# The second MLP product in token order, with the row chain behind the gates

## The reference

```python
h = tok(x)                                    # einsum bhid,oi,od->bho
h = h + attn_block(layernorm(h))              # linear attention, then the MLP:
#   x = x + attn;  h2 = ln(x)*g2 + beta2
#   x = x + gelu(h2 @ w1 + b1) @ w2 + b2      # 256 -> 1024 -> 256
h = h + ffn(layernorm(h))                     # no scale or shift in this layernorm
# ffn: logits = x @ gate_w.T (8 experts and one shared)
#      up to 4 experts a token by a sparse mixer, a cumulative top-p and a capacity
#      of 1280 tokens an expert, counted in token order
#      shared expert: silu(x @ G) * (x @ U) @ Dn, weighted by its softmax share
#      routed experts: the same with their own weights, added to the rows
```

## Time and profile before

| | busy us | share of the span |
|---|---|---|
| TensorE products | 2390.9 | 87% |
| VectorE | 1896.1 | 69% |
| GpSimd | 1566.2 | 57% |
| ScalarE | 1464.7 | 53% |

### The profile page before, as it was taken

One profiled execution on the slowest core, in us unless ns is written; L12 is line 12 of the kernel. 1 busy time (PEld: TensorE's weight loads), 2 busy tenths in 40 slices (PEclk: granted clock), 3 DMA queues, 4 the chain that ended last, 5 costly groups with the idle time before them and its releaser, 6 DMA issues. The chain is left out here.

```text
span 2740.9 us, 61192 instructions
## 1 busy us (share of the span) xinstructions
PE 2390.9 (87%) x22832; PEld 1732.9 (63%) x22832; DVE 1896.1 (69%) x4174; ACT 1464.7 (53%) x2731; POOL 1566.2 (57%) x1546
## 2 busy tenths in 40 slices
PE   4799999999999999999999858889898898985664
PEld 3588888888888888888887724444444444443553
DVE  2577777777777777777777736787777777875443
ACT  3566666666666666666666534444443344432232
POOL 1465656565666656565656523665566556656566
PEclk8999999999999999999999979999999999998787
DMA  4121111111111111111110020211121111100676
GB/s 146 43 64 61 40 64 61 61 44 61 60 61 42 42 40 44 40 44 36 47 38 14 9 98 24 78 59 50 48 84 53 50 41 50 35 9 16 128 136 100
DMA packets 115060, 152.21 MB, mean 56 GB/s; under 512 B 16537, under 2 KB 75917, under 8 KB 114768
## 3 DMA queue, kind: packets, MB, share of 16 engines
q1 hardware_dynamic: 88880, 124.46, 14.2%
q0 software_dynamic: 23808, 21.74, 4.4%
q10 hardware_dynamic: 2080, 2.10, 0.2%
...
## 5 line engine op out<-in xcount | busy, mean ns | idle before, releaser
L952 POOL TENSOR_TENSOR qkl<-fz,qkh 128x512 f16<-128x512 f32 x256 | 307.7, 1202 | 308.0 <-DVE qkh L849 303.8
L1806 POOL DMA_INDIRECT slot_dram<-xt,slot_u x256 | 257.5, 1006 | 74.9 <-issue 74.7
L521 PE MATMUL pF<-nh,qk_h 128*128 128x256 f16 x1024 | 281.3, 275 | 8.1 <-DVE nl L836 4.4
L522 PE MATMUL pF<-nh,qk_l 128*128 128x256 f16 x1024 | 280.6, 274 | 0.0
L523 PE MATMUL pF<-nl,qk_h 128*128 128x256 f16 x1024 | 280.5, 274 | 0.0
L964 POOL TENSOR_TENSOR ol<-on,oh 128x256 f16<-128x256 f32 x256 | 171.9, 672 | 153.5 <-ACT oh L786 153.5
L971 POOL TENSOR_TENSOR kvl<-kvacc,kvh 128x260 f16<-128x260 f32 x192 | 150.2, 782 | 107.7 <-ACT kvh L794 107.7
L763 ACT ACTIVATE sh<-sm 128x512 f16<-128x512 f32 x256 | 159.3, 622 | 84.5 <-DVE sm L872 84.5
L1786 POOL TENSOR_TENSOR al<-az,ah 128x512 f16<-128x512 f32 x64 | 79.2, 1238 | 215.8 <-DVE ah L1579 215.8
L846 DVE SCALAR_TENSOR_TENSOR fz<-pF,ez 128x512 f32<-128x512 f32 x256 | 175.3, 685 | 30.5 <-ACT ez L746 28.4
L740 ACT ACTIVATE rz<-pF 128x512 f32<-128x512 f32 x256 | 150.8, 589 | 84.5 <-PE pF L523 79.9
...
...
## 6 DMA issues: line engine op xcount, KB each, us to landing
xs<-in_x SPq DMA_DIRECT2D x128, 256.0 KB, 2.6
...
```

The source lines that it names most:

```text
L521: pe.matmul(out, wh, mh, start=first, stop=False, skip_group_check=True)
L522: pe.matmul(out, wl, mh, start=False, stop=False, skip_group_check=True)
L952: nc.gpsimd.tensor_tensor(qkl[:, pair:pair + 2, cols], fz[:, n % 2, :, :], qkh[:, pair:pair + 2, cols], ALU.subtract).then_inc(fl_ready, 1)
L1806: nc.gpsimd.indirect_dma_start(io["slot_dram"], bass.IndirectOffsetOnAxis(slot_u[:, c, k:k + 1], 0), xt[:, i % 2, c, :], None, bounds_chec ...
```

## The change

- `w2` puts tokens on partitions: the stationary side is `gh`/`gl` of a chunk of tokens, the moving side a row of `w2`, into pY as the down product does. The residual goes in by eight fp32 products of `hx` with `ident_w` (64 times the identity) at the head of w2. The biases and scales are as before.
- ScalarE copies the sum out of PSUM to `ht` (two buffers). VectorE takes mean and variance of each token there by bn_stats and bn_aggr. `mean3`, `var3`, `hp`, `xc3`, `sq3` and `turn_sums` go. rs3 has four columns, not 512.
- `xn` is made in token order, its high half by ScalarE and its low half by GpSimd straight into `xt` (three buffers). `turn_rows` now transposes from `xt` to the feature order, and ScalarE copies that to `xf`, from where gates and logits read.
- The order: `rstd3` stands behind `scale2`, `norm3` between gates 1 and 2, the low halves (`low3`) behind gates 2 and 3, then `rows_ahead` with `hx` and `x1` of later sequences. `turn_rows` half 0 stands between k = 1 and k = 2 of the down product, half 1 behind it.
- The explicit load of the exp and ln tables moves from `rstd3` to `logits`.

```diff
-        hp = sb("hp", [DT, T])
-        xc3, sq3, ln3, rs3, xn = sb("xc3", [DT, T]), sb("sq3", [DT, T]), sb("ln3", [T]), sb("rs3", [T]), sb("xn", [DT, T])
-        xnh, xnl = sb("xnh", [DT, T], F16), sb("xnl", [DT, T], F16)
-        xt = sb("xt", [2, CH, ROW], U32)
-        ht = sb("ht", [CH, D])
+        ht = sb("ht", [2, CH, D])
+        st3, mv3 = sb("st3", [CH, 6]), sb("mv3", [CH, 2])
+        ln3, rs3, xn = sb("ln3", [CH]), sb("rs3", [CH]), sb("xn", [CH, D])
+        xt = sb("xt", [XT, CH, ROW], U32)
+        xf = sb("xf2", [2, DT, T], F16)
+        xnh, xnl = xf[:, 0, :, :], xf[:, 1, :, :]
...
+                s["sums3"](i)
...
+                s["rstd3"](i)
...
-                s["mean3"](i, before)
...
-                    s["gate_up"](i - 1, after, (1, 2))
-                s["var3"](i)
+                    s["gate_up"](i - 1, after, (1,))
+                s["norm3"](i)
+                if before:
+                    s["gate_up"](i - 1, after, (2,))
+                s["low3"](i, 0)
                 if before:
                     s["gate_up"](i - 1, after, (3,))
-                s["rstd3"](i)
+                s["low3"](i, 1)
+                s["rows_ahead"](i)
...
-                    s["down"](i - 1)
-                s["turn_rows"](i, before)
+                    s["down"](i - 1, (0, 1))
+                s["turn_rows"](i, before, 0)
+                if before:
+                    s["down"](i - 1, (2, 3))
+                s["turn_rows"](i, before, 1)
...
-                s["turn_sums"](i)
...
+                if js[0] == 0:
+                    if i == 1:
+                        pe.wait_ge(ht_ready, 2)
+                    elif i >= 2:
+                        pe.wait_ge(ob_ready, count(i, CH, -CH))
+                    pe.wait_ge(hx_ready, count(i, DT, DT))
+                    for c in range(CH):
+                        toks = slice(c * P, (c + 1) * P)
+                        for t in range(DT):
+                            at = c // 2 * D + t * P
+                            mm = pe.matmul(pY[c % 2][:, at:at + P], hx[:, t, toks], ident_w[:, :], start=c < 2 and t == 0,
+                                           stop=False, skip_group_check=True)
+                    mm.then_inc(hx_added, 1)
...
+                    for c in range(CH):
+                        toks = slice(c * P, (c + 1) * P)
+                        mm = three(pY[c % 2][:, c // 2 * D:(c // 2 + 1) * D], gh[:, j, toks], gl[:, j, toks],
+                                   w2_h[:, j, :], w2_l[:, j, :], False, j == FT - 1)
...
-                for t in range(DT):
-                    mm = pe.matmul(pL[:, :], ones[:, :], hp[:, t, :], start=(t == 0), stop=(t == DT - 1))
...
+                if js[0] == 0:
+                    pe.wait_ge(xf_ready, count(i, 2, 2))
...
-            def var3(i):
-                pe.wait_ge(sq3_ready, count(i, DT, DT))
-                pe.wait_ge(xc3_ready, count(i, DT, DT))
-                for t in range(DT):
-                    mm = pe.matmul(pL[:, :], ones[:, :], sq3[:, t, :], start=(t == 0), stop=(t == DT - 1))
-                mm.then_inc(var3_done, 1)
...
+            def down(i, ks):
+                pe.wait_ge(ht_ready, 2 * SEQS if i == SEQS - 1 else count(i + 1, 2, 2))
+                for k in ks:
...
+                pe.wait_ge(xf_ready, count(i, 2, 2))
+                if i > 0:
+                    pe.wait_ge(lg_ready, count(i, 1, 0))
...
-                    pe.wait_ge(xt_ready, count(i, 2, half + 1))
-                    for c in range(2):
-                        toks = slice((2 * half + c) * P, (2 * half + c + 1) * P)
-                        for t in range(DT):
-                            w = c * DT + t
-                            mm = pe.transpose(pA[half][:, w * P:(w + 1) * P], hp[:, t, toks], ident[:, :])
-                    mm.then_inc(ht_done, 1)
+            def turn_rows(i, before, half):
+                pe.wait_ge(xnh_ready, count(i, 2, half + 1))
+                pe.wait_ge(xnl_ready, count(i, 2, half + 1))
+                if before:
+                    pe.wait_ge(az_ready, count(i, ST, 0))
+                else:
+                    pe.wait_ge(xc2_ready, count(i + 1, DT, DT))
+                    pe.wait_ge(rs2_step, count(i + 1, 2, 1))
+                bank16 = pA[half][:, :].bitcast(F16)
+                for part in range(2):
+                    for t in range(DT):
+                        for c in range(2):
+                            w = (part * DT + t) * 2 + c
+                            words = slice((part * DT + t) * P // 2, (part * DT + t + 1) * P // 2)
+                            mm = pe.transpose(bank16[:, w * P:(w + 1) * P],
+                                              xt[:, i % XT, 2 * half + c, words].bitcast(F16), ident16[:, :])
+                mm.then_inc(xt_done, 1)
...
+            def sums3(i):
+                act.wait_ge(w2_done, count(i, 1, 1))
+                if i >= 2:
+                    act.wait_ge(ob_ready, count(i, CH, -CH))
+                for b in range(2):
+                    nc.scalar.activation(ht[:, i % 2, b:CH:2, :], pY[b][:, :].rearrange("p (c n) -> p c n", c=2), ACT.Copy,
+                                         scale=1 / W2_SCALE).then_inc(ht_ready, 1)
+
+            def rstd3(i):
+                act.wait_ge(mv3_ready, count(i, CH, CH))
+                nc.scalar.activation(ln3[:, :], mv3[:, :, 1], ACT.Ln, bias=EPS).then_inc(rs3_step, 1)
+                act.wait_ge(rs3_step, count(i, 2, 1))
+                if i > 0:
+                    act.wait_ge(xn_ready, count(i, CH, 0))
+                nc.scalar.activation(rs3[:, :], ln3[:, :], ACT.Exp, scale=-0.5).then_inc(rs3_step, 1)
+
+            def norm3(i):
+                if i >= XT:
+                    act.wait_ge(rows_sent, count(i - XT + 1, 16 * CH * TOP, 0))
+                    act.wait_ge(xt_done, count(i - XT, 2, 2))
+                for half in range(2):
+                    act.wait_ge(xn_ready, count(i, CH, 2 * half + 2))
+                    nc.scalar.activation(xt[:, i % XT, 2 * half:2 * half + 2, 0:D // 2].bitcast(F16),
+                                         xn[:, 2 * half:2 * half + 2, :], ACT.Copy).then_inc(xnh_ready, 1)
...
-            def rstd3(i):
-                exp_ln_tables(nc, act)
-                act.wait_ge(var3_done, count(i, 1, 1))
-                nc.scalar.activation(ln3[:, :], pL[:, :], ACT.Ln, bias=EPS).then_inc(rs3_step, 1)
...
-
+                exp_ln_tables(nc, act)
...
-                    act.wait_ge(xt_done, count(i, 2, half + 1))
-                    if i >= 2:
-                        act.wait_ge(rows_sent, count(i - 1, 16 * CH * TOP, 0))
-                    nc.scalar.activation(xt[:, i % 2, 2 * half:2 * half + 2, 0:ROW_ID].bitcast(F16),
-                                         pA[half][:, :].bitcast(F16).rearrange("p (c n) -> p c n", c=2),
-                                         ACT.Copy).then_inc(xt_ready, 1)
-
-            def turn_sums(i):
-                for half in range(2):
-                    act.wait_ge(ht_done, count(i, 2, half + 1))
-                    if not at_start(i):
-                        act.wait_ge(ob_ready, count(i, CH, 0))
-                    nc.scalar.activation(ht[:, 2 * half:2 * half + 2, :],
-                                         pA[half][:, :].rearrange("p (c n) -> p c n", c=2), ACT.Copy).then_inc(ht_ready, 1)
+            def turn_rows(i, before, half):
+                act.wait_ge(xt_done, count(i, 2, half + 1))
+                if i > 0:
+                    act.wait_ge(gu_done, count(i, 2 * ST, 0))
+                    act.wait_ge(lg_done, count(i, 1, 0))
+                nc.scalar.activation(xf[:, :, :, half * 2 * P:(half + 1) * 2 * P].rearrange("p a t n -> p (a t) n"),
+                                     pA[half][:, :].bitcast(F16).rearrange("p (w n) -> p w n", n=2 * P),
+                                     ACT.Copy).then_inc(xf_ready, 1)
...
-                ve.wait_ge(w2_done, count(i, 1, 1))
-                ve.wait_ge(hx_ready, count(i, DT, DT))
-                if not at_start(i):
-                    ve.wait_ge(ht_done, count(i, 2, 0))
-                for m in range(DT):
-                    nc.vector.scalar_tensor_tensor(hp[:, m, :], pY[m][:, :], 1 / W2_SCALE, hx[:, m, :],
-                                                   ALU.mult, ALU.add).then_inc(hp_ready, 1)
-
-            def mean3(i, before):
-                ve.wait_ge(mean3_done, count(i, 1, 1))
-                ve.wait_ge(hp_ready, count(i, DT, DT))
-                for m in range(DT):
-                    nc.vector.tensor_tensor(xc3[:, m, :], hp[:, m, :], pL[:, :], ALU.subtract).then_inc(xc3_ready, 1)
+            def sums3(i):
+                if i > 0:
+                    ve.wait_ge(rs3_step, count(i, 2, 0))
+                    ve.wait_ge(xn_ready, count(i, CH, 0))
+                for b in range(2):
+                    ve.wait_ge(ht_ready, count(i, 2, b + 1))
+                    for c in (b, b + 2):
```

(40 more changed lines are left out.)

135 lines of the change are left out of this document (42 added, 93 removed).

## The result

The change made the kernel slower: 2784.99 us median of four runs (2783.17 to 2786.25) against 2747.65 of the kernel before beside it, ratio 1.0135 (95% interval 1.0113 to 1.0157). Forecast were 2729 and a range of 2702 to 2762. The profiled span is 2781.4 us against 2740.9.

| | before | after | difference |
|---|---|---|---|
| s of body 0 | 1646.54 | 1652.24 | +5.7 |
| to s of body 1 | 45.70 | 41.83 | -3.9 |
| to s of body 15, 14 intervals | 772.50 | 813.33 | +40.8 |
| to the end of the trace | 276.2 | 274.0 | -2.2 |

The account below looks back on a forecast made before the run. No engine is full, so waits decide. Body 0 -4.7, body 1 +1.2 and 14 intervals -15 sum to -18.5 us, from 2748 to 2729; range 2702 to 2762, its own case 2725 to 2733 at 0.40.

Parts of the forecast that it names:

- s: Moment when VectorE starts a body's row chain: hp before the change, the first bn_stats after; bodies 54.6 us apart before.
- The new chain: Row chain through gates to w1: az(0) at s+5.0, low3(1) until s+20.5, w1 between s+23.7 and s+25.4, against 25.48.
- GpSimd's queue: hx, x1 and six sends end gl(0) at s+34.5; fifth gelu waits for it, a new 2.2 us wait in w1.
- hx: Eight fp32 products with the identity at the head of w2: 2.1 us taken, bounds 1.7 and 3.0.
- C: Start of the counts on TensorE: forecast to stay at s+49.4, or s+49.9 where the mask is later.
- rival B: Nothing gained: clock lost at the new 2.2 us wait in w1, body 55.0, 2750 us; chance 0.15.
- C to s: From the counts to the next row chain: 4.0 us instead of 5.24, as TensorE hardly waits at C.
- The clock at C: Half clock at the counts gives 5.24 us from C to s, full clock 4.00; the change was to keep it full.
- Body 0: First body, without gates beside the chain: end of w2 to w1 13.0 us, not 19.8; -4.7 with hx, then +1.2 in body 1.
- The rule against the change: VectorE and GpSimd share a locked port pair: a norm3 pass meeting GpSimd would be held some 1.0 us.
- C (gate chain grows): Slower: az(0) to low3(1) grows, delaying the counts through GpSimd's queue; with 2.5 us, body 55.9, 2763 us; chance 0.25.
- A: Larger gain: fifth gelu not held, clock full in the down product, counts at s+48.2, body 52.2, 2711 us; chance 0.20.

Follow-up runs that it names:

- g4: Changed kernel with its 16 sends split 4 behind the down product, 4 in w1, 8 behind the counts, turns unmoved: 0.9903 of before.
- e12: Changed kernel with down product k 2 ahead of turn 0 and sends split 4 behind the down product, 4 in w1, 8 behind the counts: 2701.61 us, 0.9884.
- groups 1 and 3: Follow-up runs on two chips, where the kernel before took 2736.5 and 2734.6 us; on three other chips it took 2753.3, 2751.7 and 2748.0.
- e8: Changed kernel with down product k 2 ahead of turn 0, hx and x1 between the gates, six sends behind the counts: 1.0046 of before.
- e4: Changed kernel with down product k 2 ahead of the first half of turn_rows: 0.9990 of before.
- e6: Changed kernel with down product k 2 ahead of turn 0 and the six sends behind the counts: 0.9943 of before.
- e9: Changed kernel with the six sends held until the mask is cast: 1.0006 of before.
- e1: Changed kernel with the six sends beside the second MLP product held until the counts are done: 0.9992 of before.

## Why the prediction failed

- **The new chain.** Right. az(0) at s+4.3 (forecast 5.0; statistics took 1.8 us in place of 2.6), the `xt` write held 1.16 and the `tid` write free, az(2) at s+13.8 (14.5), az(3) ends at s+17.96 (17.75), low3(1) at s+20.8 (20.5), w1 at s+25.2 (between 23.7 and 25.4, the end with the clock lost in the 3.66 us wait).
- **GpSimd's queue.** Right. gl(0) at s+34.9 (34.5), the fifth gelu released by it, product 6 at s+35.7 (35.4). The wait in front of it is 0.91 us and not 2.2 where w1 itself starts late (bodies 3 to 8), and 2.60 in bodies 10 to 14. g4 and e12 show the same limit from the other side.
- **hx.** 16 records of 0.11 us spacing, 1.8 us from the first to w2: the lower bound (1.7), where 2.1 was taken.
- **C.** Right in bodies 3 to 8: s+49.8 (49.4 to 49.9). In bodies 10 to 14 it is s+51.4 to 51.6, by the clock lost behind the 2.60 us wait in w1, the mechanism of rival B.
- **C to s.** This is the step that failed. It said "TensorE hardly waits at C, so C to s is 4.0". It was read off body 1, the one body with counts in which no sends run, and left out what the six sends do to a TensorE that comes to the counts without a wait. Measured were 8.1 us in bodies 2 to 8, and 6.2 to 6.5 in bodies 9 to 14, where TensorE comes late and the stall ends at nearly the same distance from the mask. The body is 57.9, not 53.4 to 53.9. The 14 intervals were forecast at -15 us and came out at +40.8, 55.8 apart; 48.8 of it is C to s beyond 4.0, the other 7.0 lie ahead of C. Body 9 of before, with the same arrival and 4.59 us of stall, stood in the trace that the forecast was made from and wasn't looked at.
- **The clock at C.** The premise of that step fails too. It put the 1.24 us between 5.24 and 4.00 down to the half clock. The counts behind the last body show 0.63 us from mask to t1 at half clock on the chips of groups 1 and 3. So most of the 1.13 us that the bodies of before have there beyond the 0.60 of body 1 isn't the clock in the counts: they too are held by the sends. An estimate from these rows: 14 times 1.1 is 16 us, about as much as before differs between the chips (11 to 19 us). No trace of before was taken on the faster chips, so this isn't shown.
- **Body 0.** s of body 1 was to come 3.5 us earlier and came 1.8 later. The chain from the end of w2 to w1 took 14.1 us (forecast 13.0, before 19.8): 1.1. The phase begins 1.5 later (first mean at 1604.95, before 1603.42), which wasn't reckoned with, and the variance product of sequence 0 ran at half clock, 1.3. The last 1.4 weren't traced.
- **The rule against the change.** norm3 ran free of GpSimd, as its order promised. e8 shows what it would have cost: 1.44 us for its four passes, where 1.0 for one was written.
- **Rivals.** None was this one. C (gate chain grows) gave a time of 2763, but the chain didn't grow. B's mechanism, the clock lost in w1, is there in the bodies in which w1 starts early (bodies 10 to 14 of the change, e4, e6 and some of e9: TensorE waits 2.6 us and the next 3.4 us run at half clock). A's mechanism, the fifth gelu not held, is what e12 brings about: C at s+47.6 and a body of 51.9, where A said s+48.2 and 52.2.
- **Where the forecast holds without the stall.** The bodies of e1 in which the clock falls only behind the 3.7 us wait in the down product take 53.94 us, two such bodies of e9 53.6, at the upper end of the forecast of 53.4 to 53.9.

Open: why the counts are held by the sends, why this wasn't seen on two of the chips, which send lets them go, and what 1.6 us of it has to do with the form of the products. The amount of data isn't the reason: behind the last body of before the transfers come to 1 GB/s, and mask to t1 is 2.27 us. No packet of instruction fetch lies inside the stall between 1975.82 and 1980.54 (the nearest start at 1965.03 and 1982.18). The trace's records of TensorE in bodies 2 to 8 place the counts and product 7 ahead of the stall, those of bodies 9 to 14 inside it, so they don't tell which instruction is held.
